# Query and key terms split and turned inside the projection loop and kept in DRAM; routing and slot counting beside the first attention steps

## The reference

```python
xn = _layernorm(x, axis=-1)
x = x + attn(xn, Wqkv, Wout) + ffn(xn, gate_w, w11, w33, w22, sw1, sw2, sw3)

# attn: 16 heads of 16, rotary turn of q and k, causal softmax
q = q * cos + rotate_half(q) * sin
k = k * cos + rotate_half(k) * sin
scores = jnp.einsum('bhqd,bhkd->bhqk', q, k) * scale      # causal mask, softmax
out = jnp.einsum('bhqk,bhkd->bhqd', attn, v)
# ffn: 32 experts, 6 of them per token, inner width 128, and a shared expert of inner width 256
w, idx = _gate(xf, gate_w)          # sigmoid scores, best 4 of 8 groups, best 6 experts
y = jnp.einsum('tei,te,edi->td', silu(g) * u, c, w22)
shared = silu(xf @ sw1.T) * (xf @ sw3.T) @ sw2.T
```

## Time and profile before

| | us |
|---|---|
| median of 3 runs | 957.71 (954.71 to 959.66) |
| the profiled execution | 964.53 |
| its span, first to last instruction | 962.6 |
| PE busy | 869.7 (90%) |
| DVE busy | 622.8 (65%) |
| POOL busy | 527.5 (55%) |
| ACT busy | 511.2 (53%) |
| mean granted clock of PE | 0.963 of full |

### The profile page before, as it was taken

One profiled execution on the slowest core, in us unless ns is written; L12 is line 12 of the kernel. 1 busy time (PEld: TensorE's weight loads), 2 busy tenths in 40 slices (PEclk: granted clock), 3 DMA queues, 4 the chain that ended last, 5 costly groups with the idle time before them and its releaser, 6 DMA issues.

```text
span 962.6 us, 18240 instructions
## 1 busy us (share of the span) xinstructions
PE 869.7 (90%) x5601; PEld 478.6 (50%) x5602; DVE 622.8 (65%) x1271; ACT 511.2 (53%) x1222; POOL 527.5 (55%) x712
## 2 busy tenths in 40 slices
PE   5799766798989987989999999989999999999997
PEld 2366443333343432468878887753444344443344
DVE  2688936788856776755555555546688857978422
ACT  3444251255666564634445444447666677666662
POOL 2033339958979316056666666528886887830000
PEclk9899985799999999999999999989999999999998
DMA  7001002000000001037787786945552452520011
GB/s 208 1 11 39 25 4 66 1 1 2 1 2 1 2 1 50 1 106 241 218 242 227 230 244 182 126 106 72 73 72 33 58 73 31 72 34 1 9 37 45
DMA packets 55932, 70.93 MB, mean 74 GB/s; under 512 B 11552, under 2 KB 47392, under 8 KB 55840
## 3 DMA queue, kind: packets, MB, share of 16 engines
q0 software_dynamic: 19968, 31.47, 18.4%
q1 hardware_dynamic: 18976, 21.53, 7.4%
q10 hardware_dynamic: 16896, 16.78, 5.2%
HBM read 48.53 MB, written 21.23 MB: 72 GB/s over the span
## 4 chain that ended last, share of the span: by engine, by line
PE 43%; issue 40%; DVE 7%; ACT 3%; DMA 3%; SPq 2%; DVEq 1%; ACTq 0%
PE bank L1126 9%; PE bank L1111 7%; PE vector_banks L1091 6%; PE vector_banks L1191 5%; PE vector_banks L982 4%; PE vector_banks L1001 4%; DVE mpart L896 4%; PE bank L1001 2%; PE bank L1204 2%; DMA xn_all<-wexp 2%; PE vector_banks L1146 2%; ACT turned L571 2%; PE bank L982 2%; SPq L414 1%; PE bank L1017 1%
## 5 line engine op out<-in xcount | busy, mean ns | idle before, releaser
L660 ACT ACTIVATE probs<-bank 128x512 f32<-128x512 f32 (+3 forms) x640 | 313.4, 536 | 226.6 <-PE bank L1114 104.8
L896 DVE TENSOR_REDUCE mpart<-vector_banks 128x2 f32<-128x1024 f32 (+3 forms) x320 | 327.0, 1062 | 98.2 <-PE vector_banks L1091 60.4
L1111 PE MATMUL bank<-turned 99*128 99x512 bf16 (+3 forms) x640 | 208.9, 358 | 16.2 <-ACT probs L660 8.5
L1091 PE MATMUL vector_banks<-turned 96*128 96x512 bf16 (+3 forms) x640 | 185.9, 362 | 16.9 <-DVE mpart L896 12.9
L539 POOL DMA_INDIRECT turned<-normed_rows,tok_i x128 | 125.5, 981 | 96.0 <-PE vector_banks L982 79.1
L554 POOL DMA_INDIRECT res<-expert_rows,slot_i x96 | 148.5, 1547 | 41.3 <-issue 29.9
L1126 PE MATMUL bank<-probs,V 128*32 128x512 f32 (+3 forms) x1280 | 152.9, 548 | 1.7 <-ACT probs L660 1.3
L1111 PEld LDWEIGHTS bank<-turned 99*128 99x128 bf16 x640 | 58.9, 98 | 183.5 <-ACT probs L660 111.9
L1191 PE MATMUL vector_banks<-xn_all,probs 128*128 x512 | 135.4, 387 | 4.6 <-issue 2.0
L1191 PEld LDWEIGHTS vector_banks<-xn_all,probs 128*128 128x128 f32 x512 | 87.1, 190 | 17.3 <-issue 9.2
L571 ACT ACTIVATE probs<-bank 128x128 f32<-128x128 f32 (+1 forms) x256 | 83.9, 330 | 18.1 <-PE bank L1204 4.3
(11 more groups left out here) (154 smaller groups left out, 1001.9 us busy)
## 6 DMA issues: line engine op xcount, KB each, us to landing
expert_rows<-probs ACTq DMA_DIRECT2D x32, 512.0 KB
xn_all<-wexp SPq DMA_DIRECT2D x32, 384.0 KB
normed_rows<-xn_all SPq DMA_DIRECT2D x4, 512.0 KB, 3.2
turned<-normed_rows,tok_i POOLq DMA_INDIRECT x128
out<-res SPq DMA_DIRECT2D x16, 128.0 KB, 1.7
res<-x SPq DMA_DIRECT2D x1, 1536.0 KB, 9.4
res<-expert_rows,slot_i POOLq DMA_INDIRECT x96
probs<-wqkvT SPq DMA_DIRECT2D x1, 768.0 KB, 5.3
```

What stands on the lines that cost most here:

```text
L660: A(PT[v // 2 % 4][:, v % 2, 0:width], bank[A_BANK[step][0]][:, 0:width], ACT.Exp).then_inc(s["scalar_bank_read"], 1)
L896: V.tensor_reduce(mpart[:, t % TPC, 2 * j:2 * j + 2, p], ring[:, :, 0:w], AX.X, ALU.max).then_inc(s["vector_bank_read"], 1)
L1091: last = mm(ring[:, h, 0:w], q_turned(slice(0, KQ), 2 * j + h, t * P, P), k_turned(par, slice(0, KQ), 2 * j + h, p * CH, w), start=True, s ...
L1111: last = mm(ring[:, 0:CH - off], k_turned(parity(g), slice(0, KM), h, kb * P, P), q_turned(slice(0, KM), h, c * CH + off, CH - off), start ...
```

## The change

1. **Split per tile.** `qk_all`, `cat_q`, `cat_k`, `rem` and `prepare` are gone. After `rope` of a tile, POOL splits q and k of all 16 heads at once, in four instructions of 512 columns, into `split[b]`, two buffers in turn.
2. **Turn per tile.** PE turns the three terms in the projection loop two tiles later (`turn_terms`, twice a tile, 6 transposes each, in PSUM banks 7 and 0), ACT copies them to `staged` (`terms_turned`, twice a tile, 768 bf16 columns each).
3. **Through DRAM.** Per quarter of the tokens SP stores the terms to `term_rows` with 24 DMAs of 128 KB (a term goes to each of the six places that use it), waits for all, and loads chunk by chunk straight into `turned` (`load_terms`, 96 rows x 4 heads x 512 tokens, 384 KB). Groups 1 to 3 are loaded the same way later, once their buffer is free (`used`). The steps `q`, `k` and `prep` leave the order, so nothing of it turns or copies terms after the projections.
4. **Opening.** Attention's first strips come right after the last projection. The 13 pieces of the last quarter's routing and 14 pieces of slot counting (with PE's `counts`, `ranks`, `owner`, now in bank 7) are set between strips and score blocks: eight pieces in `opening`, the others two after each of the next eleven score blocks.
5. The slot table's steps (`tok`) run from key block 8 to 50 instead of 7 to 48. Temporary tiles lie in a new region, `at_first`, and `shared_down` and the terms of the last two tiles follow the opening strips.

```diff
-TOKENS_FROM, TOKENS_TO = 7, 48
+TOKENS_FROM, TOKENS_TO = 8, 50
...
+SPLIT = 3
+SLOT_TERM = ((0, 0, 1, 1, 0, 2), (0, 1, 0, 1, 2, 0))
...
-            scores += turns(g, c)
             scores += strips(g, c)
...
-    order = [step for c in range(NCH) for step in turns(0, c)]
+    chain = [("route", i) for i in range(ROUTE_PIECES)]
+    chain += [("counts",), ("slots", 0), ("ranks",)] + [("slots", i) for i in range(1, 7)]
+    chain += [("owner",)] + [("slots", i) for i in range(7, SLOT_PIECES)]
+    order = []
+    for step in strips(0, 0):
+        order += [step, chain.pop(0)]
...
+        for _ in range(2):
+            if chain:
+                order.append(chain.pop(0))
...
+            def load_terms(kind, g, c):
+
+                at, arrived = (0, q_in[c]) if kind == 0 else ((1 + parity(g)) * HG * T, k_in[parity(g)][c])
+                sp.dma_start(QK[0:KQ, at:at + HG * T].rearrange("p (h q) -> p h q", q=T)[:, :, c * CH:(c + 1) * CH],
+                             term_rows[kind, g * HG:(g + 1) * HG, :, :, c * CH:(c + 1) * CH].rearrange("h s d t -> (s d) h t")
+                             ).then_inc(arrived, 16)
...
+            def used(g, c):
+
+                sp.wait_ge(s["scalar_bank_full"], A_AT["st", g, c, TPC * (c + 1) - 1, HG - 1] + 1)
...
+                sp.wait_ge(s["terms_read"], 2 * QT4 * (quarter + 1))
+                for kind in range(2):
+                    for place, n in enumerate(SLOT_TERM[kind]):
+                        for half in range(2):
+                            sp.dma_start(term_rows[kind, half * H // 2:(half + 1) * H // 2, place, :, quarter * CH:(quarter + 1) * CH],
+                                         staged[quarter % 2][:, n, 2 * kind + half, :]).then_inc(s["terms_stored"], 16)
+                sp.wait_ge(s["terms_stored"], 16 * STORES * (quarter + 1))
+                for kind in range(2):
+                    load_terms(kind, 0, quarter)
...
+            for t in range(NT):
+                b = t % 2
+                gp.wait_ge(s["qk_ready"], t + 1)
+                if t >= 2:
+                    gp.wait_ge(s["terms_turned"], 2 * (t - 1))
+                gp.tensor_copy(split[b][:, 0, :], qk[b][:, :])
...
+                gp.tensor_tensor(left[:, :], qk[b][:, :], split[b][:, 0, :], ALU.subtract)
...
+                gp.tensor_copy(split[b][:, 1, :], left[:, :])
...
+                gp.tensor_tensor(split[b][:, 2, :], left[:, :], split[b][:, 1, :], ALU.subtract).then_inc(s["terms_made"], 1)
...
+            def terms_turned(t, kind):
+                act.wait_ge(s["terms_turned"], 2 * t + (1 if kind else 2))
+                if t >= 2 * QT4:
+                    act.wait_ge(s["terms_stored"], 16 * STORES * (t // QT4 - 1))
+                copy(staged[t // QT4 % 2][:, :, 2 * kind:2 * kind + 2, t % QT4 * P:(t % QT4 + 1) * P],
+                     term_bank(t, kind)).then_inc(s["terms_read"], 1)
...
+            def turn_terms(t, kind):
+                pe.wait_ge(s["terms_made"], t + 1)
...
+                for n in range(SPLIT):
+                    for a in range(2):
+                        last = turn(term_bank(t, kind)[:, n, a, :], split[t % 2][:, n, (2 * kind + a) * P:(2 * kind + a + 1) * P],
+                                    identb[:, :])
...
                         if step == strips(g, c)[0]:
-                            for turned_to in turns(g, c):
...
+                            pe.wait_ge(q_in[c], 16 * (g + 1))
+                            pe.wait_ge(k_in[parity(g)][c], 16 * (g // 2 + 1))
...
             attend(opening)
...
+            turn_terms(NT - 2, 1)
+            turn_terms(NT - 2, 0)
+            shared_down(NT - 1, (NT - 1) % 2)
+            turn_terms(NT - 1, 1)
+            turn_terms(NT - 1, 0)
             attend(early)
```

346 lines of the change are left out of this document (183 added, 163 removed).

## The result

| | before | after |
|---|---|---|
| median, us | 957.79 (954.71 to 959.66) | 918.25 (916.95 to 925.86) |
| ratio | | 0.9607, 95% interval 0.9549 to 0.9665 |
| profiled execution, us | 964.53 | 916.95 |
| its span, us | 962.6 | 915.2 |
| PE busy, us | 869.7 (90%) | 832.9 (91%) |

What follows compares the result with a forecast made beforehand. PE bounds projections and late attention; from 112 to 145.4 us no engine is full. Terms +11.2 - 28.4 + 6.5 + 5 - 1 - 11 - 15 = -32.7 us take the median 957.7 to 925 us, range 908 to 948.

Steps and rivals of the forecast that it cites:

- Turning in the projection loop: Projections: 12 transposes for each of 14 tiles on PE, which has no idle time; 0.8 us a tile, +11.2 us.
- The helpers: Projection loop: ACT's copies and POOL's casts and subtractions, with DVE, stay under 6.6 us a tile; costed at nothing.
- The gap: Between projections and first strips (33.4 us): only the last hidden row's path, 5 us, stays; -28.4 us.
- The first strips: Opening of attention, 14.0 us before: eight routing pieces and the last shared add come between them; +6.5 us.
- the blocks behind: First score blocks: remaining routing and counting pieces beside them cost between +2.2 and +9.6; middle taken, +5 us.
- The turning steps: Attention: early loses 20 steps, late 28; -11 us for early and -15 us for late.
- the second reading: Late attention: pace of a stretch without turning, 0.769 us a block against 0.814, gives 14.5 us over 322 blocks.
- Rival 1: Projections: badly overlapping stores make a round 41 us, ACT stops 30 us at tile 12, then PE; 955 us, chance 0.14.
- Rival 2: Attention: turning steps were not the limit, half or none of the 26 us comes; say 945 us, chance 0.11.
- Rival 3: Slow start: DVE's chain all exposed (+4.6 more), PE at 1.2 GHz some 10 us longer; 939 us, chance 0.12.
- Rival 4: More than the sum: upper ends for early and late, full clock from the first score blocks; 908 us, chance 0.13.

Runs made afterwards that it cites:

- ones_later: Changed kernel with POOL's memset of the rows of ones waiting until the first four normed tiles are there: 912.59 us, ratio 0.9536.
- chain_ahead: On top of ones_later, all 27 routing and counting pieces, last shared add and last two tiles' terms ahead of the first strip again: 923.28 us, ratio 0.967.
- late_full_steps: Changed kernel with 32 turning steps of groups 2 and 3 put back, with bank ring turns and copies on ACT or DVE: 941.36 us, ratio 0.9852.
- late_pe_only: Changed kernel with only the PE transposes of groups 2 and 3 put back (32 steps of 8), without copies or ring turns: 935.49 us, ratio 0.9771.
- stores_twice: On top of ones_later, each store of a term goes out a second time, to a DRAM tensor nobody reads: 931.13 us, ratio 0.9748.
- control: The changed kernel measured again, unchanged, as reference: 918.68 us, ratio 0.9605.

## Why the prediction was right, and where its sizes were off

**Turning in the projection loop: right.** +0.8 us a tile was forecast, +0.78 measured, in a stream without idle time. The helpers cost nothing, as said.

**The start: a cost that was missing.** The change was read part by part, but of the rows of ones only their transfer was considered, not the memset that makes them. 6.1 us of the median (ones_later). The last hidden row is reached 15.4 us later: 10.9 for 14 tiles, 6.2 for the late normed rows (first projection at 17.61 in place of 11.43 us), less 1.7. The rest lies in the first tiles, where the kernel before ran the projections of a whole tile at the lower clock (36.35 to 42.89 us, 6.5 us for what later takes 4.4) and the changed one only a part of one.

**The gap: right**, -28.1 to -28.4 us as forecast. chain_ahead puts the routing and counting part of it back.

**The first strips: too dear by 4.5 us.** The sum added all of the eight pieces' 5.6 us and the shared add to 14.0. But the earlier trace rows already had DVE busy only 9.3 of the 14.0 us there; the pieces took up most of that idle time (13.0 of 16.0 us busy now). For the blocks behind, the same question was answered with the middle between "all hidden" and "none", and that was right (+6.0 for +5). The error in the first strips and the missing start cancelled, so that the first score block stands at 148.75 us, where 148.7 was forecast: a landmark that fits does not confirm its terms.

**The turning steps: right in mechanism, too cheap by a quarter.** The sum had 26 us for 48 steps, 0.54 each. late_full_steps gives 0.71, of which PE's share is 0.53. So 48 steps are some 34 us, 8 more than forecast, if early's cost the same; by the traces' 0.65 to 0.7 they are 31 to 34. The error lies in the choice of price: the lower end, 0.45 us in a stream, is what PE's transposes cost beside nothing else, and the upper, 19.6 us for late's 28, was 0.70 and nearly exact. I let the second reading, the stretch of the earlier trace rows, pull the value down to 15. That stretch has no turning steps, but it is no clean pace: it holds 22 strips against 19 in the changed kernel, where it lasts 34.17 us in place of 36.90. That makes 0.9 us for each of these wide strips, and the strips were not in the sum at all. late_pe_only and late_full_steps bear it out: there the stretch has 22 strips and no steps again, and takes 36.89 us in both. The order, spreading them by goals over whatever else there is, has moved three from `late` into `early`. With both: late -28 x 0.71 - 2.7 = -22.6 (measured -23.8), early -20 x 0.71 + 2.7 - 4.7 = -16.2 (measured -17.5).

**The rivals.** Rival 1 did not occur; the stores had 11 us to spare, and stores_twice shows that its mechanism was right. Rival 2 is refuted by late_pe_only. Rival 3 is not seen: the stretches at low clock are 0.73 and 0.92, as before. Rival 4 gave the right sign for early and late, but full clock in the first score blocks did not come.

**In medians**: -32.7 forecast; -8 for the steps' price, +6 for the memset, -4.5 for the first strips make -39.2, and -39.5 were measured. That agreement is closer than the numbers allow: the interval of the ratio is 5.6 us to either side, control gives 38.5, and the steps' price alone is good to some 5 us. And part of the forecast's nearness was luck, since the missing memset and the dear first strips nearly cancelled. The other differences between the two profiled executions (the 4.7 us stall, the shorter end) are largely differences between executions: the time from the last `oT` copy to the last instruction varies from 11.1 to 13.7 us over the traces of this study, with no relation to the change.

## What to carry to other kernels

Price a removed step by its busy time with the waits around it, and before a stretch without the step is taken as the clean pace, count everything else that stands in it: an order spread by goals moves other work when steps leave it. Look at every instruction of a change on every engine, the set-up ahead of the loop too: one long memset at the start cost 6 us here. Work that must be done on a second engine beside attention was cheapest here spread one piece at a time, up to the point where the next engine in the chain, here POOL with its one-hot rows, began too late.

## What the runs showed of the hardware

- A POOL memset of 3 partitions x 8192 bf16 takes 6.92 us and holds a DVE TENSOR_SCALAR of 128 x 4 float32 in SBUF until it ends (6.39 us in place of 0.17), but not TENSOR_TENSOR of the same size (0.16).
- 24 stores of 128 KB whose DRAM side is 8 x 16 rows go at a DMA share of 0.50 and take 19.7 us, with 8 packets under way most of the time; as 128 rows of one stride they go at 0.72 and take 14.4 us, with 16.
- In a full stream of float32 matmuls on PE, six bf16 transposes of 128 x 128 delay the next matmul by 0.33 us, and the float32 group behind them takes 0.05 us longer than before (1.03 us where 0.97 stood, 0.91 where 0.86 did).
- One execution of 14 traced had a stall of 5.07 us on ACT and 3.19 on DVE at the same time, with no semaphore of the kernel behind it; its cause is not known.
